# One block for combine, norm, gate products and tables at the attention's head; the last combine stores by steps; routing counts by scans

## The reference

```python
x = x + 0.5 * ffn(layernorm(x))
x = x + attention(layernorm(x))
x = x + 0.5 * ffn(layernorm(x))

def ffn(x):                       # 8 experts, 2 chosen per token, 256 -> 896 -> 256
    topk_w, topk_idx = top_k(softmax(x @ gate_w), 2)      # weights divided by their sum
    rows = tokens sorted by expert
    h = silu(ragged_dot(rows, w1)) * ragged_dot(rows, w3)
    out = ragged_dot(h, w2)
    return sum over k of topk_w[k] * out at the token's place for k

def attention(x):                 # gated delta rule, 16 key heads, 32 value heads of 128
    q, k, v, z = split(x @ W_qkvz);  b, a = split(x @ W_ba)
    q, k, v = silu(causal convolution over 4 tokens);  q, k l2-normed
    g = -exp(A_log) * softplus(a + dt_bias);  beta = sigmoid(b)
    state = exp(g) * state;  state += k (v - k state) beta;  core = q state   # per token
    return (rmsnorm(core) * norm_weight * silu(z)) @ W_out
```

## Time and profile before

| what | value |
|---|---|
| median of 3 runs | 3226.09 us (3223.53 to 3227.19) |
| the profiled execution's own time | 3226.4 us |
| its span, first to last instruction | 3224.7 us |
| mean granted PE clock | 0.928 of full |
| PE busy | 2757.1 us, 86% |
| DVE busy | 1943.3 us, 60% |
| ACT busy | 1380.5 us, 43% |
| POOL busy | 671.4 us, 21% |

### The profile page before, as it was taken

The page is one execution under the profiler, slowest core; times in us unless marked ns, Lnnn a source line. Parts: engine busy times, 40 slices in busy tenths (PEclk is TensorE's granted clock), DMA queues, the critical chain, the costliest instruction groups (busy, mean ns, idle before and its releaser), DMA issues. The chain is left out here.

```text
span 3224.7 us, 58916 instructions
## 1 busy us (share of the span) xinstructions
PE 2757.1 (86%) x19218; PEld 2040.5 (63%) x19219; DVE 1943.3 (60%) x3720; ACT 1380.5 (43%) x4437; POOL 671.4 (21%) x959
## 2 busy tenths in 40 slices
PE   2699992556999999999999999999999983699992
PEld 2366661433677777777777777777777772366661
DVE  3122223478898898798798898898886544122222
ACT  0111110233566666566566566666665550111110
POOL 3100004132122222222222222222221112200003
PEclk7799996677999999999999999999999996799996
DMA  5122201145544544544544544545543312122202
GB/s 183 44 94 95 96 26 57 48 149 159 171 141 148 169 151 140 166 152 136 169 152 136 172 150 144 168 146 161 151 130 102 104 46 90 48 95 90 98 27 85
DMA packets 371258, 385.86 MB, mean 120 GB/s; under 512 B 214980, under 2 KB 285508, under 8 KB 371012
## 3 DMA queue, kind: packets, MB, share of 16 engines
q1 hardware_dynamic: 356420, 321.82, 32.6%
q0 software_dynamic: 14592, 60.83, 5.4%
HBM read 239.03 MB, written 143.52 MB: 119 GB/s over the span
## 5 line engine op out<-in xcount | busy, mean ns | idle before, releaser
L480 PE MATMUL f_ps_up<-f_wbuf,f_xgT 128*128 x1248 | 499.1, 543 | 5.4 <-issue 3.4
L575 DVE TENSOR_TENSOR f_h<-f_h,f_ps_up 128x448 f32<-128x448 f32 x156 | 97.0, 621 | 555.0 <-ACT f_h L549 555.0
L549 ACT ACTIVATE f_h<-f_ps_up 128x448 f32<-128x448 f32 x156 | 84.8, 544 | 635.0 <-PE f_ps_up L480 635.0
L480 PEld LDWEIGHTS f_ps_up<-f_wbuf,f_xgT 128*128 128x128 f32 x1248 | 231.2, 192 | 189.1 <-issue 184.8
L1156 PE MATMUL at_bank<-xnT,at_w_qk 128*128 128x512 f32 x512 | 273.9, 664 | 63.6 <-DVE at_qk L1467 57.6
L1467 DVE SCALAR_TENSOR_TENSOR at_qk<-at_bank,at_taps_qk,at_qk 128x510 f32<-128x510 f32 (+2 forms) x384 | 285.0, 744 | 60.9 <-ACT at_qk L1341 51.5
L1467 DVE SCALAR_TENSOR_TENSOR at_vT<-at_bank,at_taps_v,at_vT 128x510 f32<-128x510 f32 (+2 forms) x384 | 280.6, 744 | 36.4 <-ACT at_vT L1348 27.3
L1321 PE MATMUL at_bank<-at_w_out,at_yT 128*128 128x256 f32 x1024 | 260.1, 399 | 37.8 <-issue 31.5
L502 PE MATMUL f_ps_y<-f_wbuf,f_hT 128*128 x1092 | 248.8, 380 | 1.6 <-DVE f_hT L579 1.6
L1169 PE MATMUL at_bank<-xnT,at_w_vz 128*128 128x512 f32 x512 | 235.1, 602 | 15.6 <-DVE at_qk L1467 11.9
L1727 POOL TENSOR_SCALAR at_small<-at_small 128x4 f32<-128x4 f32 x64 | 18.3, 285 | 1089.2 <-ACT at_squares L1375 1089.2
(11 more groups left out here) (216 smaller groups left out, 5570.4 us busy)
## 6 DMA issues: line engine op xcount, KB each, us to landing
f_wbuf<-in_L_ffn_w_dram POOLq DMA_DIRECT2D x48, 896.0 KB, 8.0
at_steps_e<-steps_kept SPq DMA_DIRECT2D x64, 512.0 KB, 6.0
pt_kept<-at_pt_made SPq DMA_DIRECT2D x64, 512.0 KB, 3.1
mt_kept<-at_mt_made SPq DMA_DIRECT2D x64, 512.0 KB, 4.5
at_mt<-mt_kept SPq DMA_DIRECT2D x64, 512.0 KB, 5.1
at_pt<-pt_kept SPq DMA_DIRECT2D x64, 512.0 KB, 4.8
qk_kept<-at_qk SPq DMA_DIRECT2D x64, 256.0 KB, 3.0
ks_kept<-at_ks_made SPq DMA_DIRECT2D x64, 256.0 KB, 2.1
```

The costliest lines, as they stand in the source:

```text
L480: last = te.matmul(ps_up[hf][w][:, 0:MH], xgT[b][:, k, :], wbuf[:, bass.ds(off + (w * WSIZE + k * M + hf * MH), MH)], start=(k == 0), stop ...
L575: v.tensor_tensor(part, part, ps_up[hf][1][:, 0:MH], ALU.mult).then_inc(h_ready, 1)
```

## The change

It does four things.

1. The combine leaves `build_ffn`. The slots and weights of a token (`routed`) are now kept by `build`, and the next part does the combine: the attention's head, or at the end `build_combine_and_store`. `end_part` thus clears the feed-forward's semaphores ahead of the combine.
2. `attention_front` replaces combine, norm and tables at the attention's head by one block, in four groups of four tiles, with 16 gather buffers. POOL issues the gathers of groups 0 and 1, then partition_broadcast, then for each group the rstd (power of 4 columns), with the gathers of groups 2 and 3 behind the rstd of 0 and 1. DVE adds, takes moments and shifts the group before. PE turns a group and then projects the one before it. ACT does all copies to xnT. DVE's splits of a and b are waited for once. SP issues the attention's first weight loads here (`begin_loads`), and waits for the store of the steps at the end of the block.
3. The last combine stores x in eight steps of two tiles, each as soon as its four additions are done.
4. The running totals of the routing are made by one scan over (expert, tile) with a mask that restarts it at each expert, and the experts' starts by one scan of 8. Three memsets move ahead of the wait for the logits.

```diff
+                    link(v.memset(base[:, 0:1], 0.0))
+                    link(v.memset(carry[:], 1.0))
+                    link(v.memset(carry[:, :, 0], 0.0))
...
                     dve.wait_ge(ranked, 1)
-                    link(v.tensor_copy(totals[:], ps_rank[:, 1]))
-                    link(v.memset(before[:, 0, :], 0.0))
-                    for t in range(NT):
-                        link(v.tensor_tensor(before[:, t + 1, :], before[:, t, :], totals[:, t, :], ALU.add))
-
-                    link(v.tensor_scalar(tiles_i[:], before[:, NT, :], float(P - 1), None, ALU.add))
+                    link(v.tensor_copy(totals[:], ps_rank[:, 1].rearrange("p t e -> p e t")))
+                    link(v.tensor_tensor_scan(reached_by[:].rearrange("p e t -> p (e t)"), carry[:].rearrange("p e t -> p (e t)"),
+                                              totals[:].rearrange("p e t -> p (e t)"), 0.0, ALU.mult, ALU.add))
+
+                    v.tensor_tensor(totals[:], reached_by[:], totals[:], ALU.subtract).then_inc(chain, 1)
+                    n[0] += 1
+                    link(v.tensor_scalar(tiles_i[:], reached_by[:, :, NT - 1], float(P - 1), None, ALU.add))
                     link(v.tensor_scalar(tiles_i[:], tiles_i[:], 7, None, ALU.arith_shift_right))
                     link(v.tensor_copy(tiles_f[:, 0:E], tiles_i[:]))
-                    link(v.memset(base[:, 0:1], 0.0))
-                    for e in range(E):
-                        link(v.tensor_tensor(base[:, e + 1:e + 2], base[:, e:e + 1], tiles_f[:, e:e + 1], ALU.add))
-
-                    link(v.tensor_tensor(slots[:], before[:, 0:NT, :], ps_rank[:, 0], ALU.add))
+                    link(v.tensor_tensor_scan(base[:, 1:E + 1], c["ones"][:, 0:E], tiles_f[:, 0:E], 0.0, ALU.mult, ALU.add))
+
+                    link(v.tensor_tensor(slots[:], totals[:].rearrange("p e t -> p t e"), ps_rank[:, 0], ALU.add))
...
+def build_combine_and_store(nc, c, x, routed, rows_out, out):
...
+            @block.sync
+            def _(sp):
+                rows = out.rearrange("b (c p) d -> p (b c) d", p=P)
+                for g in range(NT // 2):
+                    sp.wait_ge(added, 4 * g + 4)
+                    sp.dma_start(rows[:, 2 * g:2 * g + 2, :], x[:, 2 * g:2 * g + 2, :]).then_inc(c["out_stored"], 16)
+                sp.wait_ge(c["out_stored"], 16 * (NT // 2))
...
-def attention_tables(nc, c, xnT, tab, W_ba, A_log, dt_bias, steps_kept, steps_stored):
-
+        build_combine_and_store(nc, c, x, pending, rows_out, out)
...
+                begin_loads(sp)
                 sp.wait_ge(rows_ready, 1)
                 sp.dma_start(steps_kept.rearrange("(k p) t -> p k t", p=ROWS_G), rows_e[0:ROWS_G]).then_inc(steps_stored, 16)
+                sp.wait_ge(steps_stored, 16)
...
+                def gather(group):
+                    for n in range(8 * group, 8 * group + 8) if pending else ():
+                        t, k = n // 2, n % 2
+                        at_least(pool, added, n - ring + 1)
+                        nc.gpsimd.indirect_dma_start(
+                            out=yg[n % ring][:], out_offset=None, in_=rows_out,
+                            in_offset=bass.IndirectOffsetOnAxis(ap=slot_of[:, t, k:k + 1], axis=0),
+                        ).then_inc(gathered[n % ring], 16)
+
+                def scale(group):
+                    part = slice(4 * group, 4 * group + 4)
+                    pool.wait_ge(moments_done, 4 * group + 4)
+                    nc.gpsimd.tensor_scalar(rstd[:, part], mv[:, part, 1], LN_EPS, None, ALU.add).then_inc(rstd_done, 1)
+                    pool.wait_ge(rstd_done, 2 * group + 1)
+                    nc.gpsimd.tensor_tensor(rstd[:, part], rstd[:, part], c["minus_half"][:, part], ALU.pow).then_inc(rstd_done, 1)
+
+                gather(0)
+                gather(1)
                 pool.wait_ge(loaded, 48)
                 nc.gpsimd.partition_broadcast(row_all[:].rearrange("p a n -> p (a n)"),
                                               rows[:].rearrange("p a n -> p (a n)"), P).then_inc(spread, 1)
+                for group in range(4):
+                    scale(group)
+                    if group < 2:
+                        gather(group + 2)
...
+                def turn(group):
+                    pe.wait_ge(xn_ready, 4 * group + 4)
+                    at_least(pe, copied, 2 * (group - 1))
                     for k in range(KD):
-                        last = nc.tensor.matmul(ps_ba[t // 8][:, t % 8, :], xnT[:, k, P * t:P * t + P], w_ba[:, k, :],
-                                                start=(k == 0), stop=(k == KD - 1))
-                last.then_inc(ba_done, 1)
+                        for t in range(4):
+                            last = nc.tensor.transpose(turned[group % 2][k][:, P * t:P * t + P],
+                                                       xn[:, 4 * group + t, P * k:P * k + P], c["ident"][:])
+                        last.then_inc(turned_ready, 1)
+
+                def project(group):
+                    pe.wait_ge(loaded, 48)
+                    pe.wait_ge(copied, 2 * group + 2)
+                    for t in range(4 * group, 4 * group + 4):
+                        for k in range(KD):
+                            last = nc.tensor.matmul(ps_ba[t // 8][:, t % 8, :], xnT[:, k, P * t:P * t + P], w_ba[:, k, :],
+                                                    start=(k == 0), stop=(k == KD - 1))
+                    last.then_inc(ba_done, 1)
+
+                for group in range(4):
+                    turn(group)
+                    if group:
+                        project(group - 1)
+                project(3)
...
+                def copy(group):
+                    for k in range(KD):
+                        act.wait_ge(turned_ready, 2 * group + k + 1)
+                        nc.scalar.copy(xnT[:, k, 512 * group:512 * group + 512], turned[group % 2][k][:]).then_inc(copied, 1)
+
+                copy(0)
+                copy(1)
                 act.wait_ge(spread, 1)
                 nc.scalar.activation(row_all[:, 0, :], row_all[:, 0, :], ACT.Exp).then_inc(e_done, 1)
+                copy(2)
+                copy(3)
...
+                def add(group):
+                    for i in range(8 * group, 8 * group + 8) if pending else ():
+                        t, k = i // 2, i % 2
+                        dve.wait_ge(gathered[i % ring], 16 * (i // ring + 1))
+                        at_least(dve, added, i)
+                        v.scalar_tensor_tensor(out=x[:, t, :], in0=yg[i % ring][:], scalar=weight_of[:, t, k:k + 1],
+                                               in1=x[:, t, :], op0=ALU.mult, op1=ALU.add).then_inc(added, 1)
+
+                def moments(group):
+                    part = range(4 * group, 4 * group + 4)
+                    if pending:
+                        dve.wait_ge(added, 8 * group + 8)
+                    for t in part:
+                        v.bn_stats(stats[:, t, :], x[:, t, :]).then_inc(stats_done, 1)
+                    for t in part:
+                        dve.wait_ge(stats_done, t + 1)
+                        v.bn_aggr(mv[:, t, :], stats[:, t, :]).then_inc(moments_done, 1)
+
+                def shift(group):
+                    dve.wait_ge(moments_done, 4 * group + 4)
+                    dve.wait_ge(rstd_done, 2 * group + 2)
+                    for t in range(4 * group, 4 * group + 4):
+                        v.tensor_scalar(xn[:, t, :], x[:, t, :], mv[:, t, 0:1], rstd[:, t:t + 1],
+                                        ALU.subtract, ALU.mult).then_inc(xn_ready, 1)
+
+                def split(k):
                     src = ps_ba[k][:].rearrange("p t (k c v) -> p k t c v", c=2, v=HV)
                     ts = slice(8 * k, 8 * k + 8)
                     for h in range(HV):
-
-                        link(v.tensor_scalar(b[:, :, ts, h], src[:, :, :, 0, h], -1.0, 80.0, ALU.mult, ALU.min))
+                        v.tensor_scalar(b[:, :, ts, h], src[:, :, :, 0, h], -1.0, 80.0, ALU.mult, ALU.min).then_inc(chain, 1)
                         dt = row_all[:, 1, :].rearrange("p (k v) -> p k v", v=HV)[:, :, h]
-                        link(v.tensor_tensor(a[:, :, ts, h], src[:, :, :, 1, h],
-                                             dt.unsqueeze(2).to_broadcast([P, NK, 8]), ALU.add))
-
+                        v.tensor_tensor(a[:, :, ts, h], src[:, :, :, 1, h],
+                                        dt.unsqueeze(2).to_broadcast([P, NK, 8]), ALU.add).then_inc(chain, 1)
+                        n[0] += 2
+
+                for group in range(4):
+                    add(group)
+                    moments(group)
+                    if group:
+                        shift(group - 1)
+                shift(3)
+                dve.wait_ge(spread, 1)
+                for k in range(2):
+                    dve.wait_ge(ba_done, 2 * k + 2)
+                    split(k)
+                dve.wait_ge(chain, n[0])
...
```

(5 more changed lines are left out.)

163 lines of the change are left out of this document (81 added, 82 removed).

## The result

The changed kernel took 3207.64 us in the median of five runs (3205.74 to 3209.73), the kernel before 3226.09 in five runs on the same chip (3223.12 to 3229.48). The ratio is 0.9943, 95% interval 0.9928 to 0.9958: faster by 18.4 us, where 17.9 had been forecast. The profiled execution is the lowest of the five, 3205.74, with a span of 3204.0.

What follows compares the result with a forecast made beforehand. Three serial places bound the changed stretches, one engine working while the rest waits, with POOL's gather issuing bounding the combine. Gains 3.3 + 5.2 + 4.1 + 5.6 = 18.2 us took the profiled 3226.4 to 3208.2, range 3200 to 3215.

Steps and rivals of the forecast that it cites:

- 1.6 for the clock: Attention's opening: PE starting while its clock is still at full saves 1.6 us; bounds 0 and 1.6.
- Clears: Semaphore clears after each feed-forward, moved ahead of the gathers and still on the path: 2.5 us.
- Head: Attention's head, combine to table chain: chain starts at 589.7 instead of 593.0, 3.3 us gained.
- the exchange back: Head, POOL between gathers 16 and 17: returning from broadcast code to arithmetic code costs 8.2 us.
- Start of the attention: Opening of the attention block: columns already loaded and PE at full clock, together 5.2 us gained.
- The 3.6 for the columns: Attention's opening: PE starts 0.1 us after the block opens instead of at 616.1, 3.6 us gained.
- Scans: Routing counts: scans replace 29 small chained instructions, 4.1 us gained in the second feed-forward, nothing in the first.
- End: Last combine and store: 5.4 us after the last add against 11.0, clears moved ahead, 5.6 us gained.
- C: Rival, head: a code exchange pair ahead of every rstd step makes it slower than before, 3230.2 us; chance 0.04.
- B: Rival, head: POOL's code exchanges are off the path, 13.8 us more go, 3194.4 us; chance 0.07.
- A: Rival, head: PE warms up during transposes and projections, 4.6 us more go, 3203.6 us; chance 0.10.
- D: Rival, attention: its cyclic chain through spilled tiles absorbs the 5.2 us shift, 3213.4 us; chance 0.10.

Runs made afterwards that it cites:

- experiment 4: Changed kernel with the eleven first weight loads moved from the head back to the start of the attention block: 3213.88 us.
- experiment 1: Changed kernel with the two rows spread by DMA loads instead of partition_broadcast on POOL: 3196.74 us, ratio 0.9912 to the kernel before.
- experiment 5: Changed kernel with one 2 MB store behind the last addition instead of eight stepwise stores: 3215.22 us.
- experiment 6: Changed kernel with the counts in both feed-forwards done by the old chained additions instead of scans: 3212.10 us.
- experiment 7: Kernel before the change with only the scans put in, in both feed-forwards: 3227.3 us.
- experiment 2: Changed kernel with partition_broadcast moved behind the last rstd, and ACT's Exp of the decay row behind its last copy: 3188.86 us.
- experiment 9: Changed kernel with broadcast behind the last rstd and PE running project 1 before turn 2: 3189.23 us first, then 3192.90 timed, ratio 0.9900.
- experiment 11: Changed kernel with the broadcast behind the last rstd, the same program as experiment 2, timed again: 3195.22 us, ratio 0.9901.
- experiment 10: Kernel of experiment 9 with added unread 256-column matmuls keeping PE busy: 3195.32 us, ratio 0.9905.
- experiment 8: Changed kernel with only PE's head order changed, project 1 running before turn 2 instead of behind it: 3203.86 us.

## Why the prediction was right, and where it was not

The time came out 0.6 us below the forecast. The mechanisms of the head, the early loads, the scans and the end came as forecast, and the reason given for the clock did not hold. Three terms were off in size and partly made up for each other: the head gave 1.9 us more and the end 0.8 more than forecast, and 1.6 for the clock stood in the sum that most executions don't give. That the sum is so close is in part luck.

**Clears.** 1.93 and 1.94 us instead of 2.5, at the end of either feed-forward; no run shows why they are shorter than the gap they were read from.

**Head, 3.3 forecast, 5.2 measured** (1.93 - 7.15). The term that was off is the exchange back: I took the 8.2 us of the earlier trace rows, and it took 6.84 (6.8 to 7.4 in the other heads that have it there). That is 1.4 of the 1.9; the clears give 0.6, and the way there took 0.3 more, which the rest of the head makes up. The mechanism is shown: removing the broadcast removed both pairs and 13.1 us, and doubling it added 13.3. That rstd behind gathers needs no pair, and memsets none, held in every kernel. The order on PE was as read: moving project 1 gave 3.6, for the 3.5 that one project lasts. The loads beside the gathers cost nothing (experiment 4), as assumed. The exchange is not needed for that slack: in experiment 1, without one, the moments of group 0 were done 6.2 us before POOL took their rstd, since the gathers of group 1 lie between.

**Start of the attention, 5.2 forecast, 5.5 measured, but only 3.7 of it belong to the change.** The 3.6 for the columns came as 3.68, and experiment 4 took 3.6 away again. The 1.6 for the clock came as 1.83 in the profiled execution: 1.99 from the first matmul to the first convolution, against 3.82 before. In experiments 5 and 6, whose code is the same from the combine up to there, it didn't: both took 3.79. Of the eight other profiled executions with these loads in the head, four took 3.79 and four 3.1 to 3.4. The windows of both kernels at that place, the changed one and that of experiment 5:

```profile
607.00:611.00 4.00, 3.62 (x8) 1.35 (x8) 1.79 (x3) 1.03 (x2) 4.00 (x6) 1.00 0.39 123
```

```profile
607.60:611.60 4.00, 3.90 (x5) 1.85 (x6) 0.48 (x1) 0.11 (x1) 3.94 (x6) 0.50 0.42 130
```

PE had been idle for 2.2 us ahead of the block in all three, so the short gap that I gave as the reason doesn't decide it, and what does is open. I should have carried this term as a bound of the range, 0 to 1.6, and not in the sum.

**Scans, 4.1 forecast, 4.16 measured** on the stretch itself (5.97 to 1.81 from the totals' copy to the slots), 3.8 and 4.25 in experiments 6 and 7, and nothing in the first feed-forward. In the profiled execution 3.39 arrived at the dispatch, because the logits took 13.20 us there and 12.72 before.

**End, 5.6 forecast, 6.4 measured** (1.94 + 0.07 - 8.41). 0.6 of the difference is the clears, the rest a store that ends 2.55 behind the last addition, where I had 2.9.

**The rivals.** C is out: two pairs, not five. B did not happen, but what it described was there to be had: 13.1 us lay in the place of the broadcast alone. A did not happen in the changed kernel (half clock from before the head to 604) and did in experiments 2, 9 and 11 for the last 3 us of the projections, worth 2.5 in experiment 2: its mechanism exists, and my argument against it, that the projections alone never did so, was too strong. D finds no support: the attention took 2048.18 us against 2047.85. But one pair of traces can't settle 5.2 us, since one program's attention differed by 10.4 us between two executions; that the shift arrives rests on the medians and on the five runs, all below the 3213.4 of D. The stretches that belong to the change sum to 18.8 (the table without its first row, the clock's 1.83 and the attention's 0.33), and the medians differ by 18.4.

**Better versions.** Each one that takes the exchanges off the path beats the kernel before: ratios of 0.9912, 0.9901 and 0.9900 in experiments 1, 11 and 9, against 0.9943 for the changed kernel. The intervals of the last two end below the changed kernel's, which starts at 0.9928; that of experiment 1 ends at 0.9935 and overlaps it, so there the gain over the changed kernel rests on the head, 13.1 us shorter. Between these three the intervals overlap, so which is best stays open; the shortest head is that of experiment 9.

## What to carry to other kernels

Before a step is moved on an engine's queue, look in the trace for what that engine must change to run it, there and back: a few hundred nanoseconds of broadcast carried 12.8 us of exchange, which delayed nothing behind the last rstd (experiment 2) and was fully paid between two gathers. Put such a step where its engine has nothing behind it that others wait for. When one program's executions differ by more than an edit is worth, compare stretches between fixed events of the trace; the head agreed to 0.1 us between two executions whose totals were 10.7 apart.

## What was not expected

The exchange on POOL costs in both directions and differs by direction: over all traces 5.5 to 6.0 us towards the broadcast, 6.8 to 7.4 back to arithmetic at the head, and 7.1 to 8.2 back in the attention (the earlier trace rows is the longest). Why the way back varies is not shown.

PE's clock differed between executions at the same place of the same code: 1.00 and 0.79 at 784 to 800 us, 1.00 and 0.50 at the opening of the attention. In the pair of experiment 11 the larger such steps cost 1.4 to 4.1 us each, and only small parts of them came back, 1.0 the largest.

In three executions (the two of experiment 9, and 10) a turn of transposes that PE had run in 2 us was taken up by ACT 2.5 to 8.7 us after its start, with ACT idle. It was not tried what removes this; in experiment 2, where a project follows the turn at once, and in experiment 8 it wasn't there.
